# The end of a graph edge stage: last eight turns written out, store rows read ahead, last node tiles inside the stage

## The reference, cut to what matters

```python
def reference(x, src, dst, edge_attr_2, edge_attr_64, ...):
    x = _layernorm(x + three_mean_layers(x, edge_index), axis=-1)
    x_send, x_recv = x[src], x[dst]
    fs, fr = _mlp(x_send, flux_...), _mlp(x_recv, flux_...)
    flux_send = jnp.einsum('ecd,ed->ec', fs.reshape(n_e, c, 2), nvec)
    flux_recv = jnp.einsum('ecd,ed->ec', fr.reshape(n_e, c, 2), nvec)
    a_ws = _mlp((x_send + x_recv) * 0.5, a_...)
    flux = 0.5 * (flux_send + flux_recv) - 0.5 * a_ws * (x_send - x_recv)
    agg = jax.ops.segment_sum(flux, dst, num_segments=12500)
    return _layernorm(x + agg, axis=-1)
```

## Time and profile before

| | |
|---|---|
| median of 3 runs | 9919.28 us |
| lowest, highest | 9918.13, 9926.27 us |
| span of the profiled execution | 7229.7 us |
| the profiled execution's own time | not given by the profile |
| median of the runs less this span | 2689.6 us |
| last gather issued (POOL) | 7154.7 us |
| last store of a window issued (SP) | 7200.0 us |
| last group's last operation (DVE) | 7222.8 us |

### The profile page before, as it was taken

How to read it: one execution, slowest core, us unless ns; L and a number is a source line. 1 busy time by engine, 2 the same in 40 slices (tenths; PEclk the granted TensorE clock), 3 DMA queues, 4 the chain that set the end, 5 groups by cost and what they waited for, 6 DMA issues and landing times. The chain is left out here.

```text
span 7229.7 us, 163080 instructions
## 1 busy us (share of the span) xinstructions
PE 5477.3 (76%) x50180; PEld 4418.6 (61%) x50180; DVE 4804.5 (66%) x9663; ACT 2615.2 (36%) x5447; POOL 5207.0 (72%) x5066
## 2 busy tenths in 40 slices
PE   2699999999999999956666666666666666666665
PEld 1699999999999999934444444444444444444443
DVE  6899898922222545466777777777777777777776
ACT  0688888810000111123333333333333333333332
POOL 4588888757776666567777777777777777777774
PEclk6799999999999999968888888888888888888887
DMA  5334333356666666656666666666666666666664
GB/s 157 118 138 141 133 136 137 136 200 228 218 223 212 225 219 225 206 142 159 169 165 165 166 169 165 166 165 168 165 166 165 169 165 165 165 169 165 165 165 107
DMA packets 598091, 1226.27 MB, mean 170 GB/s; under 512 B 328767, under 2 KB 406347, under 8 KB 580569
## 3 DMA queue, kind: packets, MB, share of 16 engines
q0 software_dynamic: 212704, 619.72, 32.9%
q1 hardware_dynamic: 369306, 570.23, 23.1%
q10 hardware_dynamic: 15471, 29.03, 1.3%
HBM read 1020.76 MB, written 197.70 MB: 169 GB/s over the span
## 5 line engine op out<-in xcount | busy, mean ns | idle before, releaser
L1826 POOL DMA_INDIRECT edge_rows<-node_table,edge_et x3224 | 3067.9, 952 | 984.6 <-issue 937.5
L1843 PE MATMUL edge_tp<-ident,edge_yc 128*128 128x128 f32 x1612 | 530.0, 349 | 1423.6 <-ACT edge_h L1926 1385.9
L855 POOL DMA_INDIRECT two_rows<-x_parts,src_at x1120 | 1077.0, 962 | 533.9 <-issue 357.6
L1342 PE MATMUL two_acc<-x_parts,win 128*128 128x192 bf16 x16072 | 1384.9, 247 | 19.0 <-issue 12.8
L1342 PEld LDWEIGHTS two_acc<-x_parts,win 128*128 128x128 fp8e4 x16072 | 1341.6, 98 | 30.8 <-issue 20.8
L1918 ACT ACTIVATE edge_yc<-edge_rows 128x512 f32<-128x512 f32 x403 | 253.7, 630 | 2676.6 <-DMA edge_rows<-node_table,edge_et 2640.8
L1843 PEld LDWEIGHTS edge_tp<-ident,edge_yc 128*128 128x128 f32 x1612 | 279.4, 173 | 1514.4 <-issue 1316.7
L1854 PE MATMUL edge_mp<-edge_h,edge_W 128*128 128x512 f32 x1612 | 1184.5, 877 | 2.0 <-ACT edge_h L1926 2.0
L1087 ACT ACTIVATE win<-one_count 128x784 fp8e4<-128x784 f32 x1312 | 1069.1, 825 | 145.0 <-PE one_count L1038 82.5
L855 POOL DMA_INDIRECT one_rows<-x_parts,src_at x560 | 868.2, 1550 | 176.9 <-issue 170.1
L2048 DVE TENSOR_REDUCE edge_ssq<-edge_sq 128x8 f32<-128x512 f32 x403 | 276.4, 686 | 996.3 <-ACT edge_sq L1933 996.3
(11 more groups left out here) (328 smaller groups left out, 7530.0 us busy)
## 6 DMA issues: line engine op xcount, KB each, us to landing
win<-adjacency SPq DMA_DIRECT2D x80, 3136.0 KB
adjacency<-win SPq DMA_DIRECT2D x41, 3136.0 KB
edge_near<-near_ids SPq DMA_DIRECT2D x403, 192.0 KB
edge_rows<-node_table,edge_et POOLq DMA_INDIRECT x3224
two_rows<-x_parts,src_at POOLq DMA_INDIRECT x1120
node_table<-two_row SPq DMA_DIRECT2D x49, 322.0 KB
edge_own<-node_table SPq DMA_DIRECT2D x46, 322.0 KB
node_sums<-edge_seg SPq DMA_DIRECT2D x806, 16.2 KB
```

Of the source, the lines that this page charges most:

```text
L855: pool.indirect_dma_start(rows[:, b % 2, e, :], None, XP.rearrange("p (j c) -> (p j) c", c=3 * C), bass.IndirectOffsetOnAxis(ap=src_at[:, ...
L1342: mm = pe.matmul(acc[b][:, half * 3 * C:(half + 1) * 3 * C], win[:, b, half, j, :].bitcast(FP8), now[:, j, :], start=(j == 0), stop=(j == ...
L1826: pool.indirect_dma_start(rows[:, h.b, t, :], None, T5, bass.IndirectOffsetOnAxis(ap=et[:, h.b, 0, t:t + 1].bitcast(I32), axis=0))\
L1843: pe.matmul(to, yc[:, h.b % 2, 2 * pr:2 * pr + 2, :].rearrange("p t c -> p (t c)"), ident[:, :], is_transpose=True, start=True, stop=False)
```

## The change

1. PE, ACT and DVE leave the loop eight turns earlier (HS - RB = 395). The turns 395 to 402 and the run-out are written out one by one by `end_turns` and `end_step`, and the lags shrink by one at turn 395 and by one more at turn 397, where a second, extra pass through the stages (`again`) takes up what the smaller lag owes. From then on PE has the lags 0, 1, 1, 3, 4 (before 1, 2, 3, 5, 6), ACT 2, 0, 0, 4, 2, 1, 5 (before 4, 1, 2, 6, 4, 3, 7), and DVE `flux` 0 and `squared`/`scale` 2 (before 1 and 4). POOL's and SP's turns stay in their loops.
2. `store` reads its row (`base_of`) ahead of its two waits, everywhere, in SP's loop too.
3. `finish` is gone. The own rows and x of the last six tiles are loaded at the end of SP's loop, ahead of its last 24 stores (966 and 192 KB); the sums of all six tiles in one load (390 KB) when the last store has landed. DVE computes three of the operations ahead of that load, then seven and the layer norm on all six tiles at once (128x384 elements instead of twice 128x192). Two outputs in place of three. The output of the last pair goes out among the last stores instead of behind them.

```diff
-JE = (J - 2 * DONE) // 2
+J0 = 2 * DONE
+JL = J - J0
...
-            finish(nc, ACC, T5, X1, out, cnt, alw, alb)
...
+def end_turns():
+
+    gained = 0
+    for c in range(HS - RB, HS + 5):
+        yield c, gained, False
+        if c in (HS - RB, HS - RB + 2):
+            gained += 1
+            yield c, gained, True
+
+def end_step(lag, least, c, gained, again):
+
+    now = max(lag - gained, least)
+    if c - now >= HS or again and now == max(lag - gained + 1, least):
+        return None
+    return ring_step(c - now)
...
             def store(h, u):
 
+                at = base_of(2 * h.c + u)
                 sp.wait_ge(sems["seg_out"], h.c + 1)
...
-                sp.dma_start(ACC[bass.ds(base_of(2 * h.c + u), NW), :], seg[u * NW:(u + 1) * NW, h.b, :]).then_inc(sems["stored"], 16)
+                sp.dma_start(ACC[bass.ds(at, NW), :], seg[u * NW:(u + 1) * NW, h.b, :]).then_inc(sems["stored"], 16)
...
             chunks(sp, step, HS, RB, DONE_LAG + 1)
+            sp.dma_start(end_own[:, :, :], tiles(T5)).then_inc(sems["end_rows_in"], 16)
+            sp.dma_start(end_x[:, :, :], tiles(X1)).then_inc(sems["end_rows_in"], 16)
             for c in range(HS - BACK, HS):
                 for u in range(2):
                     store(Chunk(0, c, RB), u)
-            out_of_pair(DONE - 1)
+                if c == HS - 7:
+                    out_of_pair(DONE - 1)
             sp.wait_ge(sems["stored"], 2 * HS * 16)
+            sp.dma_start(end_sums[:, :, :], tiles(ACC)).then_inc(sems["end_sums_in"], 16)
+            sp.wait_ge(sems["end_made"], 1)
+            sp.dma_start(out[J0 * P:(J - 1) * P, :]..., end_res[:, 0:JL - 1, :]).then_inc(sems["end_out"], 16)
+            sp.dma_start(out[(J - 1) * P:N, :], end_res[0:N_LAST, JL - 1, :]).then_inc(sems["end_out"], 16)
...
-            chunks(pe, step, HS, RB)
-            for c in range(HS, HS + 6):
+            chunks(pe, step, HS - RB, RB)
+            for c, gained, again in end_turns():
+                if c < HS and not again:
+                    turn(ring_step(c))
                 for k, run in stages:
-                    if c - k < HS:
-                        run(Chunk(0, c - k, RB))
+                    h = end_step(k, k // 2, c, gained, again)
+                    if h:
+                        run(h)
...
-            chunks(dve, step, HS, RB, DONE_LAG)
-            flux(Chunk(0, HS - 1, RB))
-            for c in range(HS - LAG, HS):
-                squared(Chunk(0, c, RB))
-                scale(Chunk(0, c, RB))
+            chunks(dve, step, HS - RB, RB, DONE_LAG)
+            fluxes, scales = HS - RB - 1, HS - RB - LAG
+            for c, gained, again in end_turns():
+                if c < HS and not again:
+                    spread(ring_step(c))
+                h = end_step(1, 0, c, gained, again)
+                if h:
+                    flux(h, h.c + 1 - scales)
+                    fluxes += 1
+                h = end_step(LAG, 0, c, gained, again)
+                if h:
+                    squared(h, fluxes - h.c)
+                if c < HS and not again:
+                    done(ring_step(c), (ring_step(c).place - DONE_PEEL) % RB)
+                if h:
+                    scale(h)
+                    scales += 1
```

More of the change, by code:

```diff
@@ L105 @@
 DONE_PEEL = RB + (HS - RB) % RB + DONE_LAG * RB
-JE = (J - 2 * DONE) // 2
 HG = JG // 2
 BLK2 = BLK + SLOTS + 8
-assert 0 < DONE < PAIRS - 1 and J == 2 * DONE + 2 * JE
+J0 = 2 * DONE
+JL = J - J0
+assert 0 < DONE < PAIRS - 1 and JL > 1 and HS - RB > DONE_PEEL
 CLEARS = 101
@@ L1962, in _ @@
             stages = ((4, squares), (1, lambda h: relu(h, 0)), (2, lambda h: relu(h, 1)), (6, take_raw), (4, root), (3, lambda h: relu(h, 2)), (7, take))
-            chunks(act, step, HS, RB, DONE_LAG)
-            for c in range(HS, HS + 7):
+            chunks(act, step, HS - RB, RB, DONE_LAG)
+            for c, gained, again in end_turns():
+                if c < HS and not again:
+                    take_y(ring_step(c))
                 for k, run in stages:
-                    if c - k < HS:
-                        run(Chunk(0, c - k, RB))
+                    h = end_step(k, 0, c, gained, again)
+                    if h:
+                        run(h)
+                if c < HS and not again:
+                    done_root(ring_step(c))
+            act.wait_ge(sems["end_squares"], 1)
+            act.activation(end_stat[:, :], end_stat[:, :], ACT.Sqrt, bias=eps4_col[:, 0:1], scale=1.0 / C).then_inc(sems["end_rooted"], 1)
         @block.vector
@@ L2025, in spread, with flux @@
                                   et[:, h.b, 1, :].unsqueeze(2).broadcast_to([P, TL, NW]), ALU.is_equal).then_inc(sems["sel_made"], 1)
-            def flux(h):
+            def flux(h, behind=LAG):
                 dve.wait_ge(gathered[h.b], 16 * TL * (h.turn + 1))
@@ L2035, in flux @@
                 if not early(h, LAG):
-                    dve.wait_ge(sems["scaled"], h.c - LAG + 1)
+                    dve.wait_ge(sems["scaled"], h.c - behind + 1)
                 dve.tensor_tensor(part[:, :, :], rows[:, h.b, :, X_F1:X_F1 + C], n1, ALU.mult).then_inc(sems["order_v"], 1)
@@ L2042, in flux, with squared @@
                 dve.tensor_tensor(to, to, part[:, :, :], ALU.add).then_inc(sems["v_made"], 1)
-            def squared(h):
+            def squared(h, ahead=LAG):
                 b = h.b % 2
@@ L2051, in squared @@
                 dve.tensor_copy(fold[:, h.b % 4, 1:3, 0], edge_of[:, bass.ds(2 * h.c, 2)]).then_inc(sems["edge_set"], 1)
-                dve.wait_ge(sems["v_made"], min(h.c + LAG, HS) if isinstance(h.c, int) else h.c + LAG)
+                dve.wait_ge(sems["v_made"], h.c + ahead)
                 if not early(h, 1):
@@ new lines, in _ @@
+            oe = Chain(dve, sems["order_e"])
+            wide = lambda col: col.broadcast_to([P, JL, C])
+            each = lambda rw: rw.unsqueeze(1).broadcast_to([P, JL, C])
+            dve.wait_ge(sems["end_rows_in"], 32)
+            oe.link(dve.tensor_tensor(by_weight[:, :, :], end_x[:, :, :], each(alw_b[:, :]), ALU.mult))
+            oe.link(dve.tensor_tensor(by_count[:, :, :], each(alb_b[:, :]), wide(cnt[:, J0:J].unsqueeze(2)), ALU.mult))
+            oe.link(dve.scalar_tensor_tensor(by_count[:, :, :], by_count[:, :, :], 4.0, end_x[:, :, :], ALU.add, ALU.mult))
@@ new lines, in _ @@
+            dve.wait_ge(sems["end_sums_in"], 16)
+            oe.link(dve.tensor_tensor(end_res[:, :, :], end_own[:, :, X_F0:X_F0 + C], wide(end_sums[:, :, S_N:S_N + 1]), ALU.mult))
+            oe.link(dve.tensor_tensor(end_mix[:, :, :], end_own[:, :, X_F1:X_F1 + C], wide(end_sums[:, :, S_N + 1:S_N + 2]), ALU.mult))
+            oe.link(dve.tensor_tensor(end_res[:, :, :], end_res[:, :, :], end_sums[:, :, S_U:S_U + C], ALU.add))
+            oe.link(dve.tensor_tensor(end_res[:, :, :], end_res[:, :, :], end_mix[:, :, :], ALU.add))
@@ L2206, in node_mlps @@
+            dve.sem_inc(sems["end_made"], 1)
 def node_mlps(nc, x, x3, X1, T4, B, start_idx, eps_col, ident, fWh, fbh, fWo, fbo, flw, flb, aWh, alw, alb):
```

90 lines of the change are left out of this document (22 added, 68 removed).

## The result

| | before | after |
|---|---|---|
| median of the runs | 9922.78 us (4 runs) | 9814.81 us (4 runs) |
| lowest, highest | 9918.13, 9949.02 us | 9794.84, 9838.62 us |
| span of the profiled execution | 7229.7 us | 9792.4 us |
| its own time | not given | 9794.84 us |
| last gather issued | 7154.7 us | 9718.6 us |

The ratio is 0.9888, with a 95% interval of 0.9862 to 0.9914: 108 us by the medians, where 23.5 were forecast and the range ended at 9888. The change is faster by more than four times what the whole end was thought to give, and by more than the 75 us that were said to be "at stake".

A forecast was written before the change was run, and what follows sets the result against it. POOL's gathers were taken to set the edge stage's pace, leaving only the 75 us behind the last gather. The terms summed to 15.0 + 8.8 - 0.3 = 23.5 us off 9919.3, so 9895.8; range 9888 to 9907.

The forecast's parts named there:

- the 2689.6 us "above" the span: Runs' median less profiled span; taken to lie outside the span, so savings carry over to the median of 9919.3 one to one.
- at stake: End of the edge stage: only the 75 us from the last gather's issue to the span's end can shrink, 0.76%.
- the same edit: SP's loop: reading a store's row ahead of its waits is worth nothing under POOL's pace, 1.2 us a turn without it.
- the term put at nothing: SP's loop: a store's row read ahead of its waits, priced at no gain because POOL's gathers cover SP.
- Term 2: SP's last eight stores: 1.6 us a step (bounds 1.4 and 2.2); last landing at 7186.4 against 7201.4.
- The first rival: Last stores: the chain does not tighten, a step stays 2.2 us, gain 19.3 us, to 9900; chance 0.13.
- Term 1: Last chunks come through PE, ACT and DVE sooner: windows at 14.9 and 20.1 us, where 23.6 and 28.7 stand.
- e3: Fourth chunk from the end; its folded window forecast 14.9 us after the last gathered rows, 15.9 at half clock.
- e0: Last chunk of the edge stage; its folded window forecast 20.1 us after its gathered rows, 21.2 at half clock.
- Term 3: Last six tiles, from last store landing to DVE's end: 12.9 us instead of 21.7, a gain of 8.8 (6.3 to 9.5).
- The rival of slow turns: Eight written-out turns: PE waiting for ACT makes them slower than the gathers' 10.05 us; at 17 us, 9951; chance 0.03.
- The early load: End of SP's loop: 1158 KB ahead of 24 stores costs zero; rival: delays the last gathers 3 us, to 9899, chance 0.05.

## Why the prediction was wrong, point by point

**The step that failed is the prediction's third paragraph, the 2689.6 us "above" the span.** They were taken as a constant outside of it, and a saving was carried over "one to one, an assumption, as no row shows what lies outside". There is no such outside: span and time differ by 2.4 us in after, and by about 2 us in every profile since. A quarter of the time missing from the span was the sign that the profiled execution was not of the kind that was timed. No rival named this.

**What hung on it: "In the loop the same edit is worth nothing, since POOL's pace covers SP; without that cover it would be a gain of 1.2 us a turn".** In short executions this holds: 2 us for 402 turns. The cover is the 267 us in a thousand that SP waits there; in long executions it is 8.6 us, and the same line, put at nothing, gives 79 us (0.9919). The condition was named and its size too large: 0.24 us a turn by the gathers, 0.20 by the medians. A read moved ahead of a wait gains at most what SP waits behind it, and that is little there. The view of waits has 8.6 us in a thousand, 0.12 us a turn, which is less than the gain. Taken instruction by instruction, 5000 to 9800 us, the steps into a store's second wait take 1.12 us a turn in the kernel before and 0.70 with the row read ahead, so the view counts too little; of these 0.42 us the turn keeps 0.25 (13.78 to 13.53). "No more is at stake" than 75 us behind the last gather fell with it.

**The direction came true in part by luck.** "Faster" was forecast for the end of the stage. In long executions the end gives little (the tails below), and the gain that made the change clearly faster is that of the term put at nothing.

**Term 2's step was right.** The stores of before with the row read ahead follow each other every 1.6 us, and so do those of after in its short execution (timeline of SP's queue, 7188.0 to 7190.5 us):

```profile
7187.87 1.93 SPq L1794 DMA_DIRECT2D node_sums<-edge_seg  x2
```

Two issues of 0.32 in 1.93 us stand 1.61 apart (before 2.21). By the rule of the Trainium skill ("DMA: Bandwidth & Descriptors", section "Anatomy of one DMA", fitted there on the gpsimd path), about 2.0 us fixed for a transfer, the step would have stayed near 2.2; on SP's queue the trace shows 1.61, so the rule does not carry over to it. The first rival, that the chain does not tighten, is refuted. But not every step is the shortest: of the last seven, four are 1.62 us, two 1.92 and one 3.22, together 13.6 us where 11.2 were forecast. The 3.22 is one late landing: of the store's sixteen parts fifteen had landed after 1.4 us, as those of its neighbours, and the last after 3.0. Such a landing, 2.2 to 3.4 us, stands among the last nine stores in eleven of the nineteen traces, with the row read ahead and (three times) without, so the read is not its cause; what is stays open.

**Term 1 was mis-sized.** Timeline of ACT, kernel after in a short execution, last copy and the last windows:

```profile
7167.39 0.63 ACT L1961 ACTIVATE edge_yc<-edge_rows 128x512 f32<-128x512 f32 x1 [3.97 <-DMA edge_rows<-node_table,edge_et]
...
7180.84 0.26 ACT L1993 ACTIVATE edge_seg<-edge_sums_ps 64x130 f32<-64x130 f32 x1
7183.91 0.26 ACT L1993 ACTIVATE edge_seg<-edge_sums_ps 64x130 f32<-64x130 f32 x1
...
7188.96 0.27 ACT L1993 ACTIVATE edge_seg<-edge_sums_ps 64x130 f32<-64x130 f32 x1 [0.81 <-PE edge_sums_ps L1932]
```

The window of e3 is ready 16.8 us behind the copy (7183.91 + 0.27), that of e0 21.8. Forecast were 14.9 and 20.1, and 15.9 and 21.2 with PE at half clock. The clock did fall on the changed order (windows of the same kernel, the columns those of the earlier trace rows):

```profile
7160.00:7167.40 7.40, 4.21 (x32) 2.54 (x33) 3.61 (x10) 2.22 (x7) 3.71 (x4) 1.00 0.51 120
7167.40:7179.00 11.60, 9.37 (x45) 5.47 (x45) 6.81 (x14) 4.39 (x10) 0.00 (x0) 0.56 0.05 11
7179.00:7189.30 10.30, 6.55 (x76) 4.18 (x75) 7.51 (x15) 3.68 (x13) 0.00 (x0) 1.00 0.03 8
```

Full clock in the turn before (PE 4.2 us busy in 7.4), 0.56 for the 11.6 us behind the last copy, full again from there. A middle between the two bounds was the wrong choice: at half clock through the part that counts, e3 came 0.9 us behind even the slower bound. Its first store is 2.2 us late and the chain 2.4 us too long: the last store stands 30.8 us behind the copy (7198.20 less 7167.39) where 26.3 were forecast. Terms 1 and 2 gave 10.5 us instead of 15.0 (last store behind last copy, before 41.3), still inside their bounds of 9.8 and 17.5.

**Term 3 was right, a little small.** DMA answer and DVE's first and last operation, kernel after, short:

```profile
edge_end_sums<-node_sums SPq DMA_DIRECT2D x1, 390.0 KB, 3.4
```

```profile
7203.13 0.56 DVE L2202 TENSOR_TENSOR edge_end_res<-edge_end_own,edge_end_sums 128x384 f32<-128x384 f32 x1 [15.15 <-DMA edge_end_sums<-node_sums]
...
7210.47 0.56 DVE L1670 TENSOR_TENSOR edge_end_res<-edge_end_res,edge_end_stat 128x384 f32<-128x384 f32 x1
```

The load of 390 KB took 3.4 us (4.6 taken; the two half loads of before 4.0), an operation of 384 elements 0.56 as read off the line between 192 and 512, and DVE 7.9 us in all (8.1). From the last landing, 7198.20 + 1.4, to DVE's end at 7211.03 it is 11.4 us for 21.7: a gain of 10.3, forecast 8.8. By the positions the three terms give some 20.5 us, and by the medians 18.7.

**The rival of slow turns, given 0.03, is what happened to the lags in long executions.** Timeline of ACT in after, long (the 10140 us chip): the copies of the last chunks, and two copies of raw sums between the first two of them.

```profile
9911.13 0.62 ACT L1961 ACTIVATE edge_yc<-edge_rows 128x512 f32<-128x512 f32 x1
...
9925.11 0.28 ACT L1987 ACTIVATE edge_raw_rows<-edge_sums_ps 128x130 f32<-128x130 f32 x1 [7.92 <-DMA x_parts<-x_parts]
...
9939.40 0.28 ACT L1987 ACTIVATE edge_raw_rows<-edge_sums_ps 128x130 f32<-128x130 f32 x1 [7.60 <-DMA x_parts<-x_parts]
...
9940.50 0.62 ACT L1961 ACTIVATE edge_yc<-edge_rows 128x512 f32<-128x512 f32 x1
...
9957.47 0.63 ACT L1961 ACTIVATE edge_yc<-edge_rows 128x512 f32<-128x512 f32 x1
...
9977.61 0.62 ACT L1961 ACTIVATE edge_yc<-edge_rows 128x512 f32<-128x512 f32 x1
...
9994.16 0.62 ACT L1961 ACTIVATE edge_yc<-edge_rows 128x512 f32<-128x512 f32 x1
...
10023.08 0.63 ACT L1961 ACTIVATE edge_yc<-edge_rows 128x512 f32<-128x512 f32 x1
```

The 14.9 us to the next copy and two of 7 stand between the last two rows. The last gather of that execution was issued at 10000.59:

```profile
10000.59 0.95 POOL L1866 DMA_INDIRECT edge_rows<-node_table,edge_et  x1 [0.30 <-issue]
```

The turn with the first extra pass takes 29.4 us (9911.13 to 9940.50), where the loop's mean is 13.5. It holds two passes through the stages, and in each ACT waits nearly 8 us for PE's window sums: PE's timeline has them done at 9916.1 and 9930.6, and ACT copies them at 9925.1 and 9939.4. The turns behind take 17.0, 20.1 (with the second extra pass) and 16.6 us, and only the last ones 7; the last copy stands 22.5 us behind the last gather. Before, on the same chip, it stood 4.1 us behind (4.0 in the short one by the earlier trace rows). From its copy on a chunk is through faster, 19.7 us where it took 30.4, but the later start takes more than that. Tails from the last gather to the end of the span, one long execution each: kernel before 78.8 us, lags only 86.9; after without the lags 63.0, after 73.8 and, here, 72.4. So the six tiles and the stores' steps shorten the tail by some 16 us, and the lags lengthen it again by 8 to 11, whereas in short executions they give 5 to 8. The medians can't tell this: for "lags only" the interval of 0.9969 to 1.0016 goes from -31 to +16 us, and near 9900 us the whole change gave 108 and 112 us where it gave 88 without the lags, with intervals of 26 to 38 us on each side. The mechanism is that of the rival, turns slower than the gathers, but the cause named for it, the clock, is not shown to be the one. The granted clock in the loop, kernel before, 5000 to 6000 us, short:

```profile
5000.00:6000.00 1000.00, 659.01 (x4477) 417.25 (x4478) 727.18 (x1598) 344.02 (x905) 757.76 (x796) 0.84 0.63 166
```

and after, 6000 to 7000 us, long:

```profile
6000.00:7000.00 1000.00, 566.49 (x3377) 351.71 (x3375) 541.08 (x1199) 269.99 (x684) 571.96 (x603) 0.76 0.47 126
```

and the four slow turns, 9911.1 to 9994.2 us, of the execution above:

```profile
9911.10:9994.20 83.10, 41.96 (x242) 25.50 (x246) 41.56 (x90) 19.94 (x51) 47.55 (x50) 0.73 0.46 121
```

The clock is 0.73 there, hardly under the 0.76 of the loop, and PE is busy for 42 of 83 us. What PE does in these turns is wait for ACT's relus of the same chunk, as the rival says, and the relus wait for PE's late signals: the transposes of turn 396 end at 9947.8, and ACT's first relu of them starts at 9955.2. (The rival's remark that the clock of 0.5 does not last in the windows was not to be read from the earlier trace rows, which end after 2.6 us; the next window of that trace, 7162.4 to 7166 us, still has 0.55, and from 7166 us on it is 1.00.)

**The early load** of own rows and x delayed nothing that shows: six tiles alone gave 8.3 us (1 to 14 by the interval), nearly all of the 8.8 that term 3 promised.

**What stays open** is what makes single instructions of SP take 0.72 us in long executions, and why a kernel has long ones on one chip and short ones on another. The early stages are longer too (the edge stage's first gather stands at 3105.8 us in before and at 4431.2 in after), so it is nothing of the edge stage. PE's late signals, 7.1 us in the median, may be the same thing as SP's long instructions or another. No run took it apart. Nor was the read-ahead tried alone at 9900 us: that it gives most of the 108 us rests on 0.9919 at 10140 us and on the lags' 0.9993 at 9898, with at most some 10 us for the six tiles.

## What to carry to other kernels

Hold the profiled span against the timed runs before reading anything else: where they differ by a quarter, the profile is of another kind of execution, and whatever is said to be covered in it may be the bound in the one that counts. So price the edits of every sequencer's stream as if it had no slack, and give that case a chance of its own; an instruction moved from behind a wait into the wait's shadow cost nothing in either kind of execution here, and gained 79 us in one of them. Where two bounds lie close, what is taken off one is given back in part by the other. And smaller lags at a loop's end are worth only what the chunk gains from its copy on, less what the turns lose in which engines now wait for each other.

## What the runs showed of the hardware that was not expected

- One program on one core ran at 7240 us on three chips, and at about 9900 or 10140 us on two others (one of them at both levels, about an hour apart). The mean granted clock was 0.88 to 0.90 in the short executions and 0.77 to 0.80 in the long ones. POOL's gathers took 0.95 us in both.
- A register read of SP has a median of 0.27 us in both, but up to 0.72 in the long ones; one instruction more of SP in a turn costs under 0.003 us in the short and 0.15 us in the long executions (2 us, by the interval 7 at most, and 374 us, for six in each of 402 turns).
- PE's signal that its window sums are done came 0.04 us after them in a short execution and 7.1 us after them in a long one of the same kernel (medians).
- A store of 32 rows landed 1.4 us after its issue whether or not SP read a register meanwhile, with single ones of 1.7 to 3.4 us, where the last of its sixteen parts was late.
